# Identity products in thirteen waits of TensorE, group ends of the second attention from PSUM, and two gate tiles ahead of the last convolved ones

## The chip, the cores and the metric

The kernel runs on one core of one Trainium2 chip. A time is the device time of one execution in microseconds (us); the span of a profiled execution is the time between its first and last recorded instruction. The core's engines are TensorE (PE; its weight loads are listed as PEld), VectorE (DVE), ScalarE (ACT), GpSimd (POOL) and SyncE (SP, which here only starts transfers). Each runs a program of its own, and the programs meet at semaphores.

## The reference

Six residual layers over 512 tokens of 512 features (`x`), with a context of 8192 rows (`ctx`). Each layer takes the layer norm of `x` and adds to `x`:

```
x = x + cross_attention(norm(x), ctx, mask)   # s0: softmax over 8192 keys, masked after the softmax
x = x + retention(norm(x))                    # s1: state = lam*state + v; q*state; norm; silu gate
x = x + quantised_ffn(norm(x))                # s2: 4-bit weight blocks, 16-bit activations scaled by a global maximum
x = x + memory_attention(norm(x), ctx)        # s3
x = x + mamba2(norm(x))                       # s4: conv of 4 taps, silu, scan, gate silu(z), rms norm
x = x + ternary_ffn(norm(x))                  # s5: 8-bit rows, ternary weights, conv of 3 taps between two products
```

In s3 the memory of a token is the context row of its highest score, and then 16 heads of 32 attend over the 512 memories:

```
qp     = q @ Wq.T;  idx = argmax(qp @ ctx.T);  mem = ctx[idx]
mk, mv = split(mem @ Wkv.T)
out    = softmax(heads(qp) @ mk.T / sqrt(32)) @ mv;  out @ Wc.T
```

In s4, `silu(z)` is the gate and `xBC = silu(conv(xBC))` holds the convolved tiles.

## The kernel before

The work is written out by hand, stage by stage (s0 to s5), one function for each engine and stage. What an engine does stands in the order of its code; it waits with `wait_ge` on a semaphore that another engine raises. All 512 tokens are in four tiles of 128 rows (`NT`), the features in four tiles of 128 (`DT`).

Wide products are made as three float16 products of 128x512 (high by high, high by low, low by high): `matmul_split`, L248 to L250, for the projections, L796 to L798 for the product of probabilities and context in s0, L1628 to L1630 for the scores of s3. PSUM has eight banks `PS[:, b, :]` of 128x512 float32.

At the end of each stage VectorE adds the product to a tile of `x` (L223, L225) and norms it (L205 to L211); `turn_tile` (L234) then has TensorE transpose the normed tile, ScalarE and VectorE copy and split it into `XT` (L288), and the first product of the next stage follows. These places, and those where a scale, a maximum or a sum crosses partitions, are where TensorE waits.

s0: `COLMAX` is spread over the partitions (L782), then the Fori over `PAIRS` makes the products, each context chunk with its low part `CLO` split by VectorE (L688). s1: the mean of the output (L950), 32 sums of one column (L956), spreads of the token scale (L961), then the float32 output product (L968). s2: turns, gate and up projections, then the down projection, which waits for the hidden tiles that VectorE quantises (L1244, L1246, the maximum; L1254, the first slice out).

s3 starts with a float32 projection (L1613). After the scores come the entries: `entry(e)` (L1681) makes logits whose maximum VectorE takes (L1555); the last entry of a head group (L1686) spreads that maximum. Then 64 units: `shifted(n)` (L1697) makes the logits of a head and a tile of 128 memories, ScalarE takes the exponential (L1504) into one of 16 buffers, and GpSimd adds them up (L1463). `weigh(b)` (L1709) multiplies four units with the values into bank 6. Four heads make a group, 16 units; at its end `sums(g)` (L1720, L1724) brings the sum of the exponentials into bank 7, and VectorE's `weighted(g)` divides bank 6 by it. In three groups of four it copies both banks first, so that TensorE may write them again; the last divides from PSUM. `weigh` lags the units by 9.

s4: after the split the small `dt` products come (40 of 16 columns, L248 to L250), then ten convolved tiles (VectorE, L1974; ScalarE's silu, L1899) and the eight gate products, which ScalarE takes out of two banks in turn with a silu (L1902). The order of ScalarE's code: all convolved silus, then all gate silus. `L2110` is a product on `IDENTB`, a bfloat16 identity, with a broadcast operand.

s5: the turns, a first projection (L2281), a scale spread over the partitions (L2296) and the second projection (L2302).

Of the kernel before, what the change touches and what calls it, by code (L numbers as in the profile page):

```python
# [29 lines left out]
P = 128  # L30
# [84 lines left out]
def perceiver_kernel(nc, a, out):  # L115
    ctx = ExitStack()
    with ctx:
# [120 lines left out]
        def keep_warm(pe, bank, rounds):  # L238


            with pe.Fori(0, rounds):
                for _ in range(8):
                    pe.matmul(PS[:, bank, 0:P], IDENT[:, :], ONES[:, :], start=True, stop=True)

# [488 lines left out]
        def s0_pe(pe):  # L733
# [50 lines left out]
            ins.then_inc(pe_marks, 1)  # L784
            with pe.Fori(0, PAIRS) as i:
                for b in range(2):
                    for j in range(CH):
                        k = (i * 2 + b) * CH + j
                        if j == 0:
                            pe.wait_ge(s0_c_hi, i * 2 + b + 1 + AHEAD_SPLIT)  # L790
                            pe.wait_ge(s0_c_lo, i * 2 + b + 1 + AHEAD_SPLIT)
                        pe.wait_ge(s0_p_hi, k + 1)
                        pe.wait_ge(s0_p_lo, k + 1)
                        for t in range(NT):
                            cols = slice(t * P, (t + 1) * P)
                            pe.matmul(PS[:, t, :], PHI[:, j, cols], CHI[:, b, j, :], start=False, stop=False)  # L796
                            pe.matmul(PS[:, t, :], PHI[:, j, cols], CLO[:, b, j, :], start=False, stop=False)  # L797
                            ins = pe.matmul(PS[:, t, :], PLO[:, j, cols], CHI[:, b, j, :], start=False, stop=False)  # L798
                        ins.then_inc(s0_pv, 1)
# [6 lines left out]
            ins.then_inc(pe_marks, 1)  # L806

# [11 lines left out]
            for t in range(NT):  # L819
# [5 lines left out]
                if t:  # L825
                    turn_tile(pe, 1, t - 1)
            turn_tile(pe, 1, NT - 1)

# [101 lines left out]
        def s1_pe(pe):  # L930
# [19 lines left out]
            pe.matmul(PS[:, 4, :], MEANW[:, :], Y[:, DT - 1, :], start=False, stop=True).then_inc(pe_marks, 1)  # L950
            pe.wait_ge(s1_gate, 2)
# [11 lines left out]
            ins.then_inc(pe_marks, 1)  # L963
            for e, rows in ((0, (0, 1)), (1, (0, 1)), (2, (0,)), (3, (0,)), (2, (1,)), (3, (1, 2, 3))):
# [295 lines left out]
        def s2_pe(pe):  # L1260
            for t in range(NT):
                turn_tile(pe, 2, t)
            for n, psum in enumerate((s2_gt_psum, s2_up_psum)):
# [16 lines left out]
            pe.wait_ge(s2_w_lo, WEIGHTS + AHEAD_LOW)  # L1280
            for g in range(F0T):
# [7 lines left out]
            for t in range(NT):  # L1289
                turn_tile(pe, 3, t)  # L1290
# [43 lines left out]
        LAG = 4  # L1334
# [174 lines left out]
        def s3_dve(dve, link):  # L1509
# [56 lines left out]
            def weighted(g):  # L1566

                dve.wait_ge(s3_pv, 4 * g + 4)
                dve.wait_ge(pe_marks, PE_MARK[f"s3_sums{g}"])
                if g < GROUPS - 1:  # L1570
                    dve.tensor_copy(DEN, PS[:, 7, :]).then_inc(s3_den, 1)
                    dve.tensor_copy(ATTT[:, g, :], PS[:, 6, :]).then_inc(s3_den, 1)
                    dve.wait_ge(s3_den, 3 * g + 2)
                    dve.reciprocal(DEN, DEN).then_inc(s3_den, 1)
                    dve.wait_ge(s3_den, 3 * g + 3)
                    dve.tensor_tensor(ATTT[:, g, :], ATTT[:, g, :], DEN, ALU.mult).then_inc(s3_attt, 1)
                    dve.wait_ge(s3_attt, g + 1)
                else:
                    dve.reciprocal(DEN, PS[:, 7, :]).then_inc(s3_den, 1)
                    dve.wait_ge(s3_den, 3 * g + 1)  # L1580
                    dve.tensor_tensor(ATTT[:, g, :], PS[:, 6, :], DEN, ALU.mult).then_inc(s3_attt, 1)
# [25 lines left out]
        def s3_pe(pe):  # L1607
# [92 lines left out]
            def weigh(b):  # L1700
# [5 lines left out]
                if m == 0 and g:  # L1706
                    pe.wait_ge(s3_den, 3 * (g - 1) + 2)
# [5 lines left out]
            def sums(g):  # L1713
# [3 lines left out]
                if g:  # L1717
                    pe.wait_ge(s3_den, 3 * (g - 1) + 1)
# [13 lines left out]
            for n in range(UNITS + 6):  # L1732
# [7 lines left out]
                if n >= 9 and n % 4 == 1:  # L1740
                    weigh((n - 9) // 4)
            sums(GROUPS - 1)
            pe.wait_ge(s3_attt, DT)
            for t in range(NT):
# [4 lines left out]
                if t:  # L1749
                    turn_tile(pe, 4, t - 1)  # L1750
            turn_tile(pe, 4, NT - 1)

# [131 lines left out]
        def s4_act(act, link):  # L1884
# [8 lines left out]
            for g in range(CVT + 2):  # L1893
                if g < CVT:
                    act.wait_ge(s4_conv_psum, g + 1)
                    act.activation(XBC[:, g, 3:], PS[:, g % 4, :], ACT.Copy, scale=1.0 / W_UP).then_inc(s4_conv_in, 1)
                if g >= 2:
                    act.wait_ge(s4_conv, g - 1)
                    act.activation(CV[:, g - 2, :], CV[:, g - 2, :], ACT.Silu).then_inc(s4_cv, 1)  # L1899
            for g in range(2 * NT):  # L1900
                act.wait_ge(s4_z_psum, g + 1)
                act.activation(ZG[:, g // 2, (g % 2) * 512:(g % 2 + 1) * 512], PS[:, 4 + g % 2, :],  # L1902
                               ACT.Silu, scale=1.0 / W_UP).then_inc(s4_z, 1)
            act.wait_ge(dve_marks, DVE_MARK["s4_la"])
# [153 lines left out]
        def s4_pe(pe):  # L2058
# [106 lines left out]
            for t in range(1, NT):  # L2165
                turn_tile(pe, 5, t)
# [103 lines left out]
        def s5_pe(pe):  # L2270
# [27 lines left out]
            ins.then_inc(pe_marks, 1)  # L2298
            for g in range(F1T - LAST):
# [69 lines left out]
```

## Time and profile before

| | before |
|---|---|
| times of three runs | 1157.22 (median), 1149.74, 1835.84 us |
| the profiled execution | 1148.62 us, span 1146.9 us |
| TensorE busy | 1020.6 us (89%), 4756 products |
| VectorE busy | 818.7 us (71%) |
| ScalarE busy | 489.6 us (43%) |
| GpSimd busy | 417.8 us (36%) |
| TensorE's mean granted clock | 0.949 of full speed |

The granted clock of the page's 40 slices reads 9999999999999999789778999999979999989898, in tenths. A busy share is an average over six stages that are limited by different engines. In the rows below, a product's length is the time that it spends in the array; the next one starts before it ends, so the rate is read from the starts.

### The profile page before, as it was taken

The page shows a single profiled execution, that of the slowest core. Times are in us where ns is not written, and L with a number is a line of the kernel's source. Part 1 is how long each engine was busy: PE and PEld are TensorE (multiplying, and loading weights), DVE is VectorE, ACT ScalarE, POOL GpSimd, SP SyncE. Part 2 cuts the span into 40 slices and gives each one's busy share as a digit, 9 for nine tenths or more (in the row PEclk, how much of TensorE's full clock was granted, in tenths as well). Part 3 has the DMA queues.
Part 4 walks back from the last instruction along what each step waited for, and adds up shares of the span by engine and source line. Part 5 has one row for each costly group of instructions (what it writes and reads, how often), then busy time and mean ns, then how long its engine had stood idle before and what let it go on. Part 6 is the DMA issues. An engine that isn't in the chain of part 4 may idle for free.

```text
span 1146.9 us, 14403 instructions
## 1 busy us (share of the span) xinstructions
PE 1020.6 (89%) x4756; PEld 483.0 (42%) x4756; DVE 818.7 (71%) x1178; ACT 489.6 (43%) x731; POOL 417.8 (36%) x229
## 2 busy tenths in 40 slices
PE   7999999899999889699457999999988779888796
PEld 3444444344444334344123444444732135466353
DVE  5476666799999266685873299999478557476796
ACT  2345555666666537047761110100035514355163
POOL 4278777200000833000020377766128820084003
PEclk9999999999999999789778999999979989999898
DMA  6145555533442535120010335446100100000001
GB/s 231 76 136 185 189 172 163 177 110 146 146 139 80 208 144 211 61 92 1 0 74 15 130 143 201 185 179 173 37 1 1 44 32 1 0 1 1 2 1 37
DMA packets 41828, 112.61 MB, mean 98 GB/s; under 512 B 4512, under 2 KB 15296, under 8 KB 35648
## 3 DMA queue, kind: packets, MB, share of 16 engines
q1 hardware_dynamic: 38592, 101.13, 25.1%
q10 hardware_dynamic: 2880, 9.96, 2.6%
q0 software_dynamic: 320, 1.05, 0.3%
q8 instruction: 21, 0.34, 0.1%
q14 instruction: 15, 0.12, 0.0%
HBM read 103.18 MB, written 7.34 MB: 96 GB/s over the span
## 4 chain that ended last, share of the span: by engine, by line
PE 74%; DVE 15%; issue 5%; ACT 3%; POOL 2%; DMA 0%; DVEq 0%; SPq 0%; POOLq 0%; ACTq 0%
PE PS L796 5%; PE PS L797 5%; PE PS L798 5%; PE PS L766 5%; PE PS L1628 5%; PE PS L768 5%; PE PS L1630 5%; PE PS L1629 5%; PE PS L767 5%; PE PS L248 4%; PE PS L249 4%; PE PS L250 4%; DVE arena L1974 2%; PE PS L738 1%; PE PS L1746 1%
## 5 line engine op out<-in xcount | busy, mean ns | idle before, releaser
L796 PE MATMUL PS<-arena 128*128 128x512 f16 x256 | 97.7, 382 | 3.6 <-DVE arena L676 3.6
L766 PE MATMUL PS<-arena 128*128 128x512 f16 x256 | 97.1, 379 | 2.0 <-DVE arena L615 2.0
L1628 PE MATMUL PS<-arena 128*128 128x512 f16 x256 | 97.1, 379 | 1.8 <-DVE arena L1512 1.8
L797 PE MATMUL PS<-arena 128*128 128x512 f16 x256 | 97.9, 382 | 0.0
L798 PE MATMUL PS<-arena 128*128 128x512 f16 x256 | 97.8, 382 | 0.0
L1630 PE MATMUL PS<-arena 128*128 128x512 f16 x256 | 97.1, 379 | 0.0
L767 PE MATMUL PS<-arena 128*128 128x512 f16 x256 | 97.1, 379 | 0.0
L1629 PE MATMUL PS<-arena 128*128 128x512 f16 x256 | 97.1, 379 | 0.0
L768 PE MATMUL PS<-arena 128*128 128x512 f16 x256 | 97.1, 379 | 0.0
L622 DVE TENSOR_TENSOR arena<-PS,arena 128x512 f32<-128x512 f32 x64 | 43.6, 681 | 58.0 <-ACT arena L546 58.0
L480 POOL TENSOR_TENSOR arena<-arena 128x2048 f16<-128x2048 f32 x16 | 66.0, 4127 | 38.5 <-ACT arena L539 38.1
L248 PE MATMUL PS<-arena 128*128 128x512 f16 x112 | 43.8, 391 | 33.4 <-DVE arena L1254 28.5
L248 PE MATMUL PS<-XT,arena 128*128 128x512 f16 x184 | 71.4, 388 | 2.0 <-DVE XT L288 2.0
L249 PE MATMUL PS<-XT,arena 128*128 128x512 f16 x184 | 71.6, 389 | 0.0
L250 PE MATMUL PS<-XT,arena 128*128 128x512 f16 x184 | 71.3, 387 | 0.0
L546 ACT ACTIVATE arena<-PS 128x512 f32 (+1 forms) x64 | 38.0, 594 | 77.5 <-PE PS L768 77.5
L563 ACT ACTIVATE arena<-arena,MASK 128x512 f16 (+1 forms) x64 | 46.2, 722 | 54.3 <-PE PS L798 49.1
L1436 POOL TENSOR_TENSOR arena<-arena 128x2048 f16<-128x2048 f32 x16 | 65.4, 4089 | 1.3
L865 POOL TENSOR_SCALAR XN<-XN 128x2048 f32<-128x2048 f32 x1 | 1.9, 1901 | 164.8 <-ACT arena L589 164.8
L1474 ACT ACTIVATE XN<-XN 128x580 f32<-128x580 f32 x16 | 10.9, 678 | 118.2 <-DMA XN<-in_WinT 118.2
L676 DVE SCALAR_TENSOR_TENSOR arena<-arena,MASK 128x512 f16<-128x512 f16 (+1 forms) x64 | 48.0, 751 | 9.6 <-ACT arena L563 8.6
L217 ACT ACTIVATE STD<-MV,EPSC 128x1 f32<-128x1 f32 x24 | 7.1, 295 | 108.2 <-DVE MV L207 108.1
(368 smaller groups left out, 2437.4 us busy)
## 6 DMA issues: line engine op xcount, KB each, us to landing
arena<-in_ctxT SPq DMA_DIRECT2D x32, 1024.0 KB, 6.4
arena<-in_ctx SPq DMA_DIRECT2D x16, 1024.0 KB, 5.2
arena<-in_w ACTq DMA_DIRECT2D x8, 1024.0 KB, 5.3
arena<-in_w SPq DMA_DIRECT2D x8, 1024.0 KB, 4.8
XN<-in_ffnGU SPq DMA_DIRECT2D x16, 384.0 KB, 3.3
XN<-in_WinT SPq DMA_DIRECT2D x16, 290.0 KB, 5.0
gu_hi<-arena SPq DMA_DIRECT2D x16, 192.0 KB, 3.4
gu_lo<-arena SPq DMA_DIRECT2D x16, 192.0 KB, 3.5
```

The lines of the kernel that those rows point to most:

```text
L248: pe.matmul(out, w_hi, m_hi, start=(c == 0), stop=False)
L249: pe.matmul(out, w_hi, m_lo, start=False, stop=False)
L250: return pe.matmul(out, w_lo, m_hi, start=False, stop=(c == n - 1))
L766: pe.matmul(bank, CHI[:, b, e, cols], QHI[:, e, :], start=(e == 0), stop=False)
L767: pe.matmul(bank, CHI[:, b, e, cols], QLO[:, e, :], start=False, stop=False)
L768: ins = pe.matmul(bank, CLO[:, b, e, cols], QHI[:, e, :], start=False, stop=(e == DT - 1))
L796: pe.matmul(PS[:, t, :], PHI[:, j, cols], CHI[:, b, j, :], start=False, stop=False)
L797: pe.matmul(PS[:, t, :], PHI[:, j, cols], CLO[:, b, j, :], start=False, stop=False)
L798: ins = pe.matmul(PS[:, t, :], PLO[:, j, cols], CHI[:, b, j, :], start=False, stop=False)
L1628: pe.matmul(bank, QHI3[:, e, cols], CHI3[:, b, e, :], start=(e == 0), stop=False)
L1629: pe.matmul(bank, QHI3[:, e, cols], CLO3[:, b, e, :], start=False, stop=False)
L1630: ins = pe.matmul(bank, QLO3[:, e, cols], CHI3[:, b, e, :], start=False, stop=(e == DT - 1))
```

## The change

A helper `fill(pe, bank, times)` makes 128x512 products of the bfloat16 identity with itself into a PSUM bank that nobody reads, and it is called in thirteen waits: 225 products in all. The down projection of s2 gets two more waits ahead of its 20. In s3, `weighted(g)` divides straight from PSUM in all four groups; `weigh` of a new group waits for the product of the division (`s3_attt`), `sums` for the reciprocal, and `weigh` lags the units by 13. In s4, ScalarE takes gate tiles 0 and 1 ahead of the convolved tiles 8 and 9.

```diff
+        def fill(pe, bank, times):
+            for _ in range(times):
+                pe.matmul(PS[:, bank, :].rearrange("p (a b) -> p a b", b=P), IDENTB[:, :],
+                          IDENTB[:, :].unsqueeze(1).to_broadcast([P, 4, P]), start=True, stop=True)
...
@@ s0, after the spread of COLMAX (L782), and after the sums (L805)
+            fill(pe, 7, 12)
...
+            fill(pe, 7, 8)
@@ s0's end
+            fill(pe, 4, 9)
             turn_tile(pe, 1, NT - 1)
+            fill(pe, 4, 4)
@@ s1, after the last mean (L950), and after the spread (L961)
+            fill(pe, 7, 6)
...
+            fill(pe, 2, 6)
@@ s2_pe
+            fill(pe, 0, 28)
             for t in range(NT):
                 turn_tile(pe, 2, t)
+            fill(pe, 4, 4)
...
             pe.wait_ge(s2_w_lo, WEIGHTS + AHEAD_LOW)
+            pe.wait_ge(s2_up, F0T)
+            pe.wait_ge(s2_tmag, NT + 2 * F0T + 2 * SLICES - 1)
+            fill(pe, 0, 20)
             for g in range(F0T):
...
             for t in range(NT):
+                fill(pe, 4 if t else 0, 8)
                 turn_tile(pe, 3, t)
@@ s3_dve, weighted(g)
-                if g < GROUPS - 1:
-                    dve.tensor_copy(DEN, PS[:, 7, :]).then_inc(s3_den, 1)
-                    dve.tensor_copy(ATTT[:, g, :], PS[:, 6, :]).then_inc(s3_den, 1)
...
+                dve.reciprocal(DEN, PS[:, 7, :]).then_inc(s3_den, 1)
+                dve.wait_ge(s3_den, g + 1)
+                dve.tensor_tensor(ATTT[:, g, :], PS[:, 6, :], DEN, ALU.mult).then_inc(s3_attt, 1)
+                dve.wait_ge(s3_attt, g + 1)
@@ s3_pe
                 if m == 0 and g:
-                    pe.wait_ge(s3_den, 3 * (g - 1) + 2)
+                    pe.wait_ge(s3_attt, g)
...
                 if g:
-                    pe.wait_ge(s3_den, 3 * (g - 1) + 1)
+                    pe.wait_ge(s3_den, g)
...
                 if e in (1, 2):
                     values(e + 1)
+                elif e:
+                    fill(pe, 6, 3)
-            for n in range(UNITS + 6):
+            for n in range(UNITS + BEHIND):
...
-                if n >= 9 and n % 4 == 1:
-                    weigh((n - 9) // 4)
+                if n >= BEHIND and n % 4 == 1:
+                    weigh((n - BEHIND) // 4)
             sums(GROUPS - 1)
+            fill(pe, 5, 18)
...
+            fill(pe, 4, 10)
             turn_tile(pe, 4, NT - 1)
+            fill(pe, 4, 4)
@@ s4_act
+            for g in range(CVT):
+                act.wait_ge(s4_conv_psum, g + 1)
+                act.activation(XBC[:, g, 3:], PS[:, g % 4, :], ACT.Copy, scale=1.0 / W_UP).then_inc(s4_conv_in, 1)
+                if g >= 2:
+                    s4_conv_silu(g - 2)
+            for g in range(2 * NT):
+                s4_gate_silu(g)
+                if g < 2:
+                    s4_conv_silu(CVT - 2 + g)
@@ s4's end
+            turn_tile(pe, 5, 1)
+            fill(pe, 4, 6)
+            turn_tile(pe, 5, 2)
+            fill(pe, 4, 18)
+            turn_tile(pe, 5, 3)
+            fill(pe, 4, 3)
@@ s5, after the spread of the scale (L2296)
+            fill(pe, 5, 7)
```

In the changed kernel the lines behind the helper stand seven or more lines later: L248 to L250 are its L255 to L257, and its L249 is the identity product.

TensorE at the end of s2, where the last two of the normed tiles are turned and s3's float32 projection (L1613, after: L1624) follows. Before:

```order
L234 MATMUL PS<-IDENT,XN 128x128 [waits ln_xn]
L234 MATMUL PS<-IDENT,XN 128x128 x3
L234 MATMUL PS<-IDENT,XN 128x128 [waits ln_xn]
L234 MATMUL PS<-IDENT,XN 128x128 x3
L1613 MATMUL PS<-XT,arena 128x512 [waits xt_ready,w_in3]
```

After:

```order
L249 MATMUL PS<-IDENTB 128x512 x8
L234 MATMUL PS<-IDENT,XN 128x128 [waits ln_xn]
L234 MATMUL PS<-IDENT,XN 128x128 x3
L249 MATMUL PS<-IDENTB 128x512 x8
L234 MATMUL PS<-IDENT,XN 128x128 [waits ln_xn]
L234 MATMUL PS<-IDENT,XN 128x128 x3
L1624 MATMUL PS<-XT,arena 128x512 [waits xt_ready,w_in3]
```

The last two turns are shown; eight identity products now stand ahead of each of the four.

TensorE in s3's units, at the start of a new head group: L1686 (after: L1697) spreads a group's maximum, L1697 (L1708) is a unit, L1709 (L1720) a weigh. Before:

```order
L1686 MATMUL PS<-IDENT,arena 4x128 [waits s3_taken_even,s3_taken_odd]
L1686 MATMUL PS<-IDENT,arena 4x128 x3
L1709 MATMUL PS<-arena 32x512 [waits s3_den,s3_p]
L1709 MATMUL PS<-arena 32x512 x3
L1697 MATMUL PS<-arena 128x512 [waits s3_p] x4
L1709 MATMUL PS<-arena 32x512 [waits s3_p]
L1709 MATMUL PS<-arena 32x512 x3
L1697 MATMUL PS<-arena 128x512 [waits s3_p] x2
```

After:

```order
L1697 MATMUL PS<-IDENT,arena 4x128 [waits s3_taken_even,s3_taken_odd]
L1697 MATMUL PS<-IDENT,arena 4x128 x3
L1720 MATMUL PS<-arena 32x512 [waits s3_p]
L1720 MATMUL PS<-arena 32x512 x3
L1708 MATMUL PS<-arena 128x512 [waits s3_p] x4
L1720 MATMUL PS<-arena 32x512 [waits s3_attt,s3_p]
L1720 MATMUL PS<-arena 32x512 x3
L1708 MATMUL PS<-arena 128x512 [waits s3_p] x2
L1708 MATMUL PS<-arena 128x512 [waits s3_p,s3_qst]
```

The first weigh of the new group stood right behind the spread and waited for the copies (`s3_den`); now the last weigh of the old group stands there, and the new group's first one, four units later, waits for the division (`s3_attt`).

TensorE at the end of s3: L1720 and L1724 (after: L1731, L1735) are the last sums, L1746 (L1760) the output product. Before:

```order
L1709 MATMUL PS<-arena 32x512 [waits s3_p]
L1709 MATMUL PS<-arena 32x512 x3
L1709 MATMUL PS<-arena 32x512 [waits s3_p]
L1709 MATMUL PS<-arena 32x512 x3
L1720 MATMUL PS<-XT,ONES 32x512 [waits s3_den,s3_acc]
L1720 MATMUL PS<-XT,ONES 32x512 x3
L1724 MATMUL PS<-arena,ONES 32x512 x4
L1746 MATMUL PS<-arena 128x512 [waits s3_attt]
```

After:

```order
L1720 MATMUL PS<-arena 32x512 [waits s3_p]
L1720 MATMUL PS<-arena 32x512 x3
L1720 MATMUL PS<-arena 32x512 [waits s3_p]
L1720 MATMUL PS<-arena 32x512 x3
L1720 MATMUL PS<-arena 32x512 [waits s3_p]
L1720 MATMUL PS<-arena 32x512 x3
L1731 MATMUL PS<-XT,ONES 32x512 [waits s3_den,s3_acc]
L1731 MATMUL PS<-XT,ONES 32x512 x3
L1735 MATMUL PS<-arena,ONES 32x512 x4
L249 MATMUL PS<-IDENTB 128x512 x18
L1760 MATMUL PS<-arena 128x512 [waits s3_attt]
```

Three weighs stand without a unit between them where two did, and 18 identity products stand between the sums and the output product.

ScalarE in s4, at the end of the convolution: L1896 (after: L1923) takes a convolved tile's input out of PSUM, L1899 (L1913) is its silu, L1902 (L1918) a gate silu. Before:

```order
L1896 ACTIVATE arena<-PS 128x512
L1899 ACTIVATE arena<-arena 128x512
L1896 ACTIVATE arena<-PS 128x512
L1899 ACTIVATE arena<-arena 128x512 x3
L1902 ACTIVATE arena<-PS 128x512 x8
L1905 ACT_TABLE_LOAD
```

After:

```order
L1923 ACTIVATE arena<-PS 128x512
L1913 ACTIVATE arena<-arena 128x512
L1923 ACTIVATE arena<-PS 128x512
L1913 ACTIVATE arena<-arena 128x512
L1918 ACTIVATE arena<-PS 128x512
L1913 ACTIVATE arena<-arena 128x512
L1918 ACTIVATE arena<-PS 128x512
L1913 ACTIVATE arena<-arena 128x512
L1918 ACTIVATE arena<-PS 128x512 x6
L1931 ACT_TABLE_LOAD
```

The first gate silu moved ahead of the last two convolved silus, the second ahead of the last.

## Rows read from the trace of the kernel before

**Rows 1.** Stretches of 1.2 GHz by windows: us, engines' busy (count), PEclk, DMA; last, full clock

```profile
216.20:219.60 3.40, 3.40 (x9) 1.31 (x10) 3.29 (x6) 2.85 (x6) 0.00 (x0) 0.53 1.01 371
387.70:390.30 2.60, 2.60 (x7) 0.95 (x8) 1.83 (x3) 0.73 (x2) 2.52 (x3) 0.50 0.99 385
417.60:421.00 3.40, 3.40 (x9) 1.29 (x10) 3.37 (x5) 2.04 (x3) 0.00 (x0) 0.52 1.01 422
463.90:468.80 4.90, 4.90 (x6) 2.18 (x7) 4.17 (x6) 0.00 (x0) 0.00 (x0) 0.50 0.02 6
492.30:496.10 3.80, 3.79 (x9) 1.33 (x10) 3.77 (x5) 0.61 (x2) 0.00 (x0) 0.50 0.00 0
585.10:588.20 3.10, 3.10 (x8) 1.13 (x9) 1.57 (x3) 3.04 (x6) 0.00 (x0) 0.50 1.01 418
628.30:632.60 4.30, 4.30 (x5) 1.82 (x6) 0.00 (x0) 1.32 (x3) 0.00 (x0) 0.50 0.74 239
848.70:853.10 4.40, 4.40 (x11) 1.43 (x12) 3.87 (x4) 1.68 (x3) 0.00 (x0) 0.50 0.00 0
921.30:926.20 4.90, 4.90 (x6) 2.18 (x7) 0.00 (x0) 0.00 (x0) 0.00 (x0) 0.50 0.00 0
945.40:950.10 4.70, 4.70 (x41) 4.22 (x40) 0.22 (x1) 0.21 (x1) 2.24 (x2) 0.50 0.01 3
984.60:987.60 3.00, 2.97 (x8) 1.05 (x9) 2.60 (x10) 0.46 (x1) 0.00 (x0) 0.50 0.00 0
1083.40:1086.60 3.20, 3.19 (x8) 1.09 (x9) 1.65 (x3) 0.60 (x2) 0.00 (x0) 0.50 0.00 0
1128.20:1131.00 2.80, 2.77 (x7) 1.03 (x8) 2.80 (x6) 2.80 (x5) 2.80 (x5) 0.50 0.00 0
240.00:340.00 100.00, 100.00 (x465) 45.18 (x463) 94.51 (x126) 65.39 (x88) 0.00 (x0) 1.00 0.38 134
```

**Rows 2.** Timeline, TensorE: start, length, instruction, [idle before <- releaser]

```profile
621.63 0.66 PE L234 MATMUL PS<-IDENT,XN 128*128 128x128 f32 x4 [2.05 <-DVE XN L211]
...
624.35 1.11 PE L234 MATMUL PS<-IDENT,XN 128*128 128x128 f32 x4 [2.06 <-DVE XN L211]
...
646.33 0.39 PE L1628 MATMUL PS<-arena 128*128 128x512 f16 x1 [1.82 <-DVE arena L1512]
...
1004.34 0.38 PE L2110 MATMUL PS<-FUTUREB,IDENTB 128*128 128x512 bf16 x1
```

**Rows 3.** Timeline at the start of stage s0's products

```profile
225.41 2.29 DVE L688 TENSOR_TENSOR arena<-arena 128x2048 f16<-128x2048 f32 x1
...
228.24 0.38 PE L796 MATMUL PS<-arena 128*128 128x512 f16 x1
```

**Rows 4.** Chain that ended last, stage s1: the spread of the scale

```profile
460.19 2.09 PE PS L961 x8
```

**Rows 5.** Timeline, TensorE, start of stage s2

```profile
487.59 3.87 PE L234 MATMUL PS<-IDENT,XN 128*128 128x128 f32 x16 [7.20 <-DVE XN L1167]
```

**Rows 6.** Timeline, VectorE, the last maximum but one of stage s2's product

```profile
577.08 1.22 DVE L1246 TENSOR_REDUCE SM<-arena 128x1 f32<-128x1024 f32 x1
```

**Rows 7.** Timeline, TensorE, gate products of stage s4

```profile
984.63 0.61 PE L248 MATMUL PS<-arena,XT 128*128 128x512 f16 x1 [2.29 <-ACT arena L1902]
```

**Rows 8.** Timeline of stage s3's group ends, TensorE and VectorE

```profile
873.43 0.68 DVE L1571 COPY arena<-PS 128x512 f32<-128x512 f32 x1
...
874.86 1.07 PE L1709 MATMUL PS<-arena 128*32 128x512 f32 x8 [0.16 <-DVE arena L1572]
...
878.13 1.12 DVE L1576 TENSOR_TENSOR arena<-arena 128x512 f32<-128x512 f32 x1
...
907.93 1.07 PE L1709 MATMUL PS<-arena 128*32 128x512 f32 x8
...
917.16 3.36 DVE L1579 RECIPROCAL arena<-PS 128x512 f32<-128x512 f32 x1 [4.51 <-PE PS L1724]
...
920.55 0.69 DVE L1581 TENSOR_TENSOR arena<-PS,arena 128x512 f32<-128x512 f32 x1
```

More of the change, by code:

```diff
@@ L1333, in perceiver_kernel @@
         MSHIFT = 64.0
-        LAG = 4
+        BEHIND = 13
         s3_clip = sem("s3_clip")
@@ L1569, in weighted @@
                 dve.wait_ge(pe_marks, PE_MARK[f"s3_sums{g}"])
-                if g < GROUPS - 1:
-                    dve.tensor_copy(DEN, PS[:, 7, :]).then_inc(s3_den, 1)
-                    dve.tensor_copy(ATTT[:, g, :], PS[:, 6, :]).then_inc(s3_den, 1)
[L1573 to L1581, printed above, removed]
+                dve.reciprocal(DEN, PS[:, 7, :]).then_inc(s3_den, 1)
+                dve.wait_ge(s3_den, g + 1)
+                dve.tensor_tensor(ATTT[:, g, :], PS[:, 6, :], DEN, ALU.mult).then_inc(s3_attt, 1)
+                dve.wait_ge(s3_attt, g + 1)
             def take_entry(e):
@@ L1892, in s4_act, with s4_conv_silu, s4_gate_silu @@
             act.activation(DTE, DTE, ACT.Ln, bias=1.0).then_inc(act_marks, 1)
[L1893 to L1900, printed above, removed]
+            def s4_conv_silu(g):
+                act.wait_ge(s4_conv, g + 1)
+                act.activation(CV[:, g, :], CV[:, g, :], ACT.Silu).then_inc(s4_cv, 1)
+            def s4_gate_silu(g):
                 act.wait_ge(s4_z_psum, g + 1)
@@ L2164, in s4_pe @@
             project_rows(3)
-            for t in range(1, NT):
-                turn_tile(pe, 5, t)
+            turn_tile(pe, 5, 1)
[4 more added lines that the diff above has]
+            fill(pe, 4, 3)
         W1B = view(53 * K, [DT, FF1], F16)
```

## Prediction

> **What bounds the kernel now.** I read the page first: TensorE is busy for most of the span, yet its granted clock is not 9 in every slice. Then the timeline of TensorE gave the starts of its 128x512 products, and the windows put a row on each stretch where they start at twice the usual distance. The reader is to see in [rows 1] that thirteen stretches have a granted clock of 0.50 to 0.53, TensorE's level of 1.2 GHz, while TensorE is busy for all of each; the last row is a stretch at 1.00 (2.4 GHz) with 465 products in 100 us, so one each 0.215 us. At the lower level it is 0.43 (8 starts in 3.4 us). All thirteen stretches follow a pause of TensorE: in [rows 2] a turn of four transposes takes 0.66 after an idle 2.05, and 1.11 after one more idle 2.06. A pause of 1.82 elsewhere left the first product at 0.39, full clock. The fourth row there is the kernel's own product on the bfloat16 identity: 0.38 at full clock, like any other, so an identity product costs 0.215 to issue.
>
> Where TensorE bounds a stretch of length L at half clock, full clock saves L/2. Everything below is summed against the profiled execution (1148.62, of which 1146.9 is span). That is 8.6 under the median of the three times, 1157.22, and 1.1 under the lowest.
>
> **The products, place by place**, in the order of [rows 1]; each first with L/2.
> - s0, 3.4: 1.7. The twelve products (2.6) lie in the wait. But the fourth key tile's second part needs the split that ends at 225.41 + 2.29 = 227.70 and TensorE reaches that tile at 228.24 [rows 3], so little over 0.4 can be kept. Bounds 0.4 and 1.7; I take 0.4, the row being right there.
> - s0 after the sums, 2.6: 1.3. Retention's start, 3.4: 1.7 (nine and four products, 2.8, in pauses ahead of and behind the last turn).
> - s1's scale, 4.9: 2.45, and half of the eight spreads of 2.09 [rows 4], 1.05, so 3.5 at most. The spreads end at 462.28 and the next product starts at 463.9: six products fit (1.3), but not at half clock (2.6), which would cost 1.0. The 32 one-column sums between the two fills keep TensorE at little work. Bounds -1.0 and 3.5; I take 1.5, between, nearer to the upper since the second fill alone shortens the pause.
> - s2's start, 3.8: 1.9. The 28 products take 6.0 of a wait of 7.20 [rows 5].
> - s2 down: 3.1 gives 1.55. The fill waits for the maximum that ends at 577.08 + 1.22 = 578.30 [rows 6]; 20 products take 4.3, or 8.6 at half clock, when they would end at 586.9 against 585.10. What is queued behind that new wait on TensorE is only the down projection, which needs a later step anyway. Bounds -1.8 and 1.55; I take 1.5.
> - s3's start, 4.3: 2.15. Eight products (1.7) ahead of each turn; the turns come each 2.72 (the starts in [rows 2]), so they fit at full clock. 2.2.
> - s3's entries, 4.4: 2.2. GpSimd is idle in that stretch and its sums, which come after, wait for the first weights, so all of it moves. VectorE is busy 3.87 of the 4.4, so at least 0.5. I take 2.2, the chain there being TensorE's.
> - s3's end, 4.9: 2.45. 18 products (3.9) beside the reciprocal and product, 3.36 + 0.69 [rows 8]: 2.4.
> - s4's first small products, 4.7: 2.35. All 40 are 16 columns, bound by weight loads (4.22 of 4.70); the transposes of [rows 2], loads with short products too, go from 1.11 to 0.66, so these halve nearly as well. 2.3, bounds 1.5 and 2.35. The convolution behind moves as a whole.
> - s5's start, 3.2: 1.6. s5 second projection, 2.8: 1.4, but its seven products (1.5, at half clock 3.0) may end 1.5 late. I take 1.2, bounds -1.5 and 1.4.
>
> **The gate tiles.** TensorE waits 2.29 for the first gate silu [rows 7], which stands behind the convolved silus 8 and 9 on ScalarE; with gate tiles 0 and 1 ahead of them the gate products run through. That removes the 2.29 and half of the 3.0 at half clock behind it: 3.8. The moved convolved silus are read by VectorE and TensorE after the gate products end, so their 0.6 each is covered.
>
> Sum of gains: 0.4 + 1.3 + 1.7 + 1.5 + 1.9 + 1.5 + 2.2 + 2.2 + 2.4 + 2.3 + 1.6 + 1.2 + 3.8 = 24.0.
>
> **The group ends of s3.** Two copies of 0.68 go, but the copies were what let TensorE on: its first weigh of the next group stood behind the second copy only (0.16 idle, at 874.86 [rows 8]). Now that weigh waits for the whole division. So each weigh is put four units later, and the last weigh of a group takes the place of the old first one, at 874.86: the sums are complete at 875.9, not before 873.43; the reciprocal (3.36) and product (0.69) end at 880.0, against 878.13 + 1.12 = 879.25. VectorE's next entries, queued behind, and through them the units that GpSimd paces, come 0.7 later, in two groups: 1.4. At the end it costs more: weigh 11 takes the slot at 907.93, ends at 909.0, the division ends at 913.1; then come weighs 12 to 15 (4 x 1.07) and the sums (2 x 1.07), 919.5 against 917.16: 2.3. Together 3.7; the two 0.7 partly hide behind GpSimd's own pace, so I take 3.1. Bounds: a loss of 3.7, and a gain of 3 x (2 x 0.68 + 0.43) = 5.4 if VectorE's shorter ends were all that counts and the later weighs nothing.
>
> The row of 0.69 is a product with one operand in PSUM, when GpSimd had no more sums; those of 1.12 had both in SBUF, beside GpSimd. The Trainium skill (SBUF — State Buffer, section "Who interferes with whom") says that a VectorE instruction with two SBUF inputs contends with a GpSimd instruction that reads SBUF, and one with at most one such input does not. By that rule the 0.69 holds beside GpSimd; without it the product would take 1.12 and two groups would end 0.4 later each, 0.8 in all. No row of this trace shows the new form beside GpSimd.
>
> Forecast: 1148.6 - 24.0 + 3.1 = 1127.7, so **1128**.
>
> **The rivals.**
> 1. VectorE is as late. In the stretches at 216, 417, 464, 492 and 849 it is busy 3.29 of 3.40, 3.37 of 3.40, 4.17 of 4.90, 3.77 of 3.80 and 3.87 of 4.40 [rows 1], so a faster TensorE would meet it. For it: these shares. Against: TensorE ran without a pause there, and much of VectorE's work is for what comes later. It takes away 0.4 + 1.7 + 1.5 + 1.9 + 2.2 = 7.7: 1135.
> 2. The group ends save: the later weighs hide behind GpSimd's pace and the shorter ends count. 1127.7 - 3.1 - 3 x 1.36 = 1120.5, so 1121. Against: the tail's 2.3 has nothing beside it.
> 3. Slower: the identity products don't bring the clock up. Then at 0.43 each the eight ahead of a turn take 3.4, with the turn's 1.11 4.5, over the 2.72 from which it decides: 1.8 x 4 = 7.3 late. The 28 take 12.0 of 7.2: 4.8 late; the 18 take 7.7 of 4.05: 3.7 late. No stretch gets faster, of the gains only 2.3 stays: 1148.6 + 7.3 + 4.8 + 3.7 + 3.1 - 2.3 = 1165; the ten fills at the entries (1.3 each) could bring 1178. Against: the row of 0.38 shows that such a product fills TensorE like a real one, and the clock was 1.00 wherever real ones ran on.
> 4. The gate tiles come no earlier, because the silu ahead of gate 0 is as late as silu 9: 3.8 stay, 1132.
>
> **How the numbers follow.** Forecast 0.45, rival 1 0.25, rival 2 0.20, rival 3 0.06, rival 4 0.04. The range goes down from rival 2 by the upper bounds at 216, s1's scale and s5 (1.3 + 2.0 + 0.2, and 1 for rounding), to 1116, and up from rival 1 by the lower bounds of s2 down, s5 and s1's spread (3.3 + 2.7 + 1.0), with 1 for the group ends, to 1143. Outside lie rival 3 and tails, about 0.15. Two per cent, about what a measurement of this kernel can tell from no change, is 1134 under the median shown, but 1126.7 under the lowest time, near which the profiled execution stands. My forecast lies between these bounds, so half of its weight and all of rival 2 and some of rival 4 are faster, rival 1 is within 2%, and slower has most of rival 3: faster 0.50, same 0.45, slower 0.05.
>
> **What would show it.** The thirteen stretches at clock 1.00, and their products 0.22 apart; the turns of s3 0.66 each; no wait of TensorE for the first gate silu; VectorE's division of the last group starting 2 to 3 after TensorE's last unit more than it did; the product from PSUM near 0.69 beside GpSimd. I am wrong if fills show 0.63 each or turns start later, or if TensorE's waits for VectorE grow by what its products lost.

## The result, and the profile after

The changed kernel took 1139.23 us (median of four, 1138.12 to 1140.73), the kernel before, in the same comparison, 1153.48 (median of four, with 1148.51 the lowest). The ratio is 0.9897, with a 95% interval of 0.9852 to 0.9941, and leaves out one slow run of before, of 1835.84: 1.0% faster. The time lies in the predicted range, but the gain is less than half of the one forecast: between the profiled executions 7.9, where 24.0 - 3.1 = 20.9 were forecast. The profiled execution took 1140.73, with a span of 1139.0 and a mean clock of 0.971 (0.949 before). In the page's row of granted clock of before, the slice at 918 to 946 us has 8 and that at 1004 to 1032 us has 9; the row under the times before has these two the other way round.

The same places as in [rows 1], in the windows of the changed kernel. The columns and the order are those of [rows 1]; the times have moved, and the eighth window holds added products as well:

```profile
218.90:220.90 2.00, 1.96 (x10) 0.93 (x11) 1.88 (x4) 1.73 (x4) 0.00 (x0) 1.00 0.93 345
390.30:391.70 1.40, 1.40 (x7) 0.63 (x8) 1.40 (x3) 0.68 (x2) 1.40 (x2) 1.00 1.01 369
420.10:422.10 2.00, 1.96 (x10) 0.92 (x11) 2.00 (x4) 0.72 (x3) 0.00 (x0) 1.00 1.01 422
465.90:468.30 2.40, 2.40 (x7) 1.14 (x7) 2.34 (x4) 0.00 (x0) 0.00 (x0) 1.00 0.00 0
491.60:493.50 1.90, 1.90 (x9) 0.87 (x10) 1.90 (x4) 0.59 (x2) 0.00 (x0) 1.00 0.00 0
582.40:584.10 1.70, 1.70 (x8) 0.77 (x9) 0.69 (x1) 1.67 (x4) 0.00 (x0) 1.00 1.00 419
623.80:625.80 2.00, 1.99 (x5) 1.04 (x6) 0.00 (x0) 1.34 (x3) 0.00 (x0) 1.00 0.60 164
841.20:844.70 3.50, 3.37 (x16) 1.18 (x15) 3.50 (x4) 1.97 (x4) 0.00 (x0) 1.00 0.00 0
925.00:927.40 2.40, 2.40 (x6) 1.20 (x7) 0.00 (x0) 0.00 (x0) 0.00 (x0) 1.00 0.02 7
946.50:949.00 2.50, 2.50 (x41) 2.27 (x40) 0.15 (x1) 0.00 (x0) 2.35 (x2) 1.00 0.00 0
981.00:982.70 1.70, 1.70 (x9) 0.75 (x8) 1.55 (x4) 0.65 (x2) 0.00 (x0) 1.00 0.00 0
1078.10:1080.20 2.10, 2.10 (x8) 0.51 (x9) 1.61 (x3) 0.57 (x2) 0.00 (x0) 1.00 0.00 0
1121.70:1123.20 1.50, 1.50 (x8) 0.73 (x8) 1.50 (x4) 1.50 (x3) 1.50 (x3) 1.00 0.00 0
```

Each of the thirteen stretches is now at 1.00, the level of 2.4 GHz. The small products of s4 (the tenth row) went from 4.70 to 2.50.

So the loss is elsewhere, and the starts of equal instructions in the two traces say where. Their difference is the lead that the changed kernel has at that point; the change of the lead across a place is what the place brought:

| place | forecast | measured |
|---|---|---|
| s0, products | 0.4 | 0.2 |
| s0, after the sums | 1.3 | 0.0 |
| s1's start | 1.7 | 1.7 |
| s1's scale | 1.5 | 1.4 |
| s2's start | 1.9 | 2.1 |
| s2 down | 1.5 | 1.1 |
| s3's start | 2.2 | 3.0 |
| s3's entries | 2.2 | 2.0 |
| s3's group ends | -3.1 | -12.4 |
| s3's output | 2.4 | 2.5 |
| s4's small products | 2.3 | 2.4 |
| gate tiles | 3.8 | 4.0 |
| s5's start | 1.6 | 1.4 |
| s5, second projection | 1.2 | 1.4 |

The gains add up to 23.1 before rounding, where 24.0 were forecast. Take off 12.4, and 2.7 that this execution was later already by the end of s0's first wait, at work that stands ahead of the first added product: 8.0, and the two profiled executions differ by 7.9.

The 12.4 is the stretch from GpSimd's first sum to VectorE's last reciprocal in s3: 62.8 before (854.3 to 917.16), 75.3 after (845.57 to 920.85). Its windows, cut at GpSimd's first sum of each group and at the end of its last sum; before:

```profile
854.30:869.00 14.70, 12.60 (x65) 3.74 (x63) 10.27 (x10) 9.44 (x17) 14.69 (x12) 0.99 0.00 1
869.00:887.90 18.90, 14.99 (x84) 4.15 (x88) 15.56 (x14) 9.55 (x17) 15.35 (x13) 1.00 0.01 1
887.90:903.80 15.90, 11.29 (x70) 2.72 (x66) 8.56 (x7) 9.33 (x17) 15.29 (x12) 1.00 0.00 1
903.80:915.00 11.20, 9.50 (x59) 1.69 (x59) 6.40 (x4) 7.29 (x12) 10.39 (x8) 1.00 0.12 25
```

and in the changed kernel:

```profile
845.60:860.30 14.70, 11.22 (x55) 3.34 (x55) 10.91 (x10) 9.39 (x17) 14.70 (x13) 1.00 0.00 1
860.30:883.20 22.90, 18.75 (x84) 4.75 (x88) 13.15 (x11) 9.56 (x17) 14.94 (x13) 0.78 0.00 1
883.20:902.30 19.10, 15.07 (x70) 3.14 (x66) 6.98 (x5) 9.34 (x17) 14.90 (x13) 0.74 0.01 2
902.30:914.40 12.10, 8.55 (x41) 1.32 (x33) 4.05 (x2) 4.93 (x9) 9.87 (x8) 0.78 0.00 1
```

Where no group ends, nothing changed: 14.7 and 14.7, GpSimd without a pause. Each group that contains an end is longer, by 4.0, 3.2 and 0.9, and the tail behind the last sum by another 4.3 (6.4 against 2.2). GpSimd's busy time is the same (some 55), so it waits (14.4 in these four windows, 5.0 before), and TensorE's clock, 0.99 to 1.00 in this whole stretch before, falls to 0.74 to 0.78 from the second window on. Over the whole stretch TensorE is busy 60.1 with the 286 products that took it 50.3 before. The timeline of TensorE has the pauses; one at each of the three group ends:

```profile
873.22 1.04 PE L1692 MATMUL PS<-arena 96*128 96x512 f16 x2 [3.54 <-DVE arena L1581]
...
893.60 1.94 PE L1720 MATMUL PS<-arena 128*32 128x512 f32 x8 [1.97 <-DVE arena L1591]
...
913.19 1.94 PE L1720 MATMUL PS<-arena 128*32 128x512 f32 x8 [2.41 <-DVE arena L1591]
```

L1591 is the product of the division, L1581 the shift row that is queued behind it on VectorE, L1720 the first weigh of the next group, 1.94 long at half clock where the weigh at 874.86 in [rows 8] took 1.07 after waiting 0.16. The entry of the first group end waited for the shift row before as well:

```profile
880.02 0.61 PE L1681 MATMUL PS<-arena 96*128 96x512 f16 x2 [2.70 <-DVE arena L1562]
```

That pause grew by 0.8 only. What grew more is how late the row comes: 12.2 after GpSimd's first sum of the group (860.27 to 872.49), 10.3 before (869.03 to 879.29).

Two places brought little or nothing for another reason. In s0 the products run through at full clock, and then TensorE waits for VectorE's split:

```profile
230.80 0.38 PE L804 MATMUL PS<-arena 128*128 128x512 f16 x1 [1.34 <-DVE arena L695]
```

The other is s0 after the sums. The timeline of the changed kernel there, GpSimd and VectorE:

```profile
404.81 4.07 POOL L879 TENSOR_TENSOR arena<-arena 128x2048 f16<-128x2048 f32 x1
...
407.26 1.89 DVE L211 TENSOR_SCALAR XN<-X,MV,RSTD 128x512 f32<-128x512 f32 x1
```

The projections got their 1.3, but the first norm behind them now takes 1.89 and ends at 409.15, just after GpSimd's subtraction of weights (408.88), and the lead at the turn behind it is what it was ahead of the sums.

### The profile page after: what moved, and what is told of

Its sections match the earlier page's. It is cut to its first block, busy times and chain, and to the rows that moved or that the text cites. A ratio compares the mean times of both kernels' runs of the same rounds, so it can differ in the third digit from the quotient of the medians.

```text
span 1139.0 us, 14848 instructions
## 1 busy us (share of the span) xinstructions
PE 1055.0 (93%) x4981; PEld 498.2 (44%) x4981; DVE 813.6 (71%) x1172; ACT 490.0 (43%) x731; POOL 415.6 (36%) x229
## 4 chain that ended last, share of the span: by engine, by line
PE 77%; DVE 13%; issue 4%; ACT 3%; POOL 1%; DMA 0%; DVEq 0%; SPq 0%; ACTq 0%; POOLq 0%
PE PS L773 5%; PE PS L774 5%; PE PS L775 5%; PE PS L1639 5%; PE PS L1641 5%; PE PS L1640 5%; PE PS L255 5%; PE PS L257 5%; PE PS L256 5%; PE PS L804 5%; PE PS L805 5%; PE PS L806 5%; PE PS L745 1%; PE PS L1720 1%; PE PS L2311 1%
## 5 line engine op out<-in xcount | busy, mean ns | idle before, releaser
L773 PE MATMUL PS<-arena 128*128 128x512 f16 x256 | 97.7, 382 | 2.0 <-DVE arena L622 2.0
L1639 PE MATMUL PS<-arena 128*128 128x512 f16 x256 | 97.0, 379 | 1.8 <-DVE arena L1531 1.8
L804 PE MATMUL PS<-arena 128*128 128x512 f16 x256 | 97.0, 379 | 1.6 <-DVE arena L695 1.3
L774 PE MATMUL PS<-arena 128*128 128x512 f16 x256 | 97.8, 382 | 0.0
L775 PE MATMUL PS<-arena 128*128 128x512 f16 x256 | 97.7, 381 | 0.0
L1640 PE MATMUL PS<-arena 128*128 128x512 f16 x256 | 97.0, 379 | 0.0
L1641 PE MATMUL PS<-arena 128*128 128x512 f16 x256 | 97.0, 379 | 0.0
L805 PE MATMUL PS<-arena 128*128 128x512 f16 x256 | 97.0, 379 | 0.0
L806 PE MATMUL PS<-arena 128*128 128x512 f16 x256 | 97.0, 379 | 0.0
L249 PE MATMUL PS<-IDENTB 128*128 128x512 bf16 x225 | 57.7, 401 | 21.9 <-DVE SM L1259 21.9
L255 PE MATMUL PS<-XT,arena 128*128 128x512 f16 x184 | 69.7, 379 | 0.6 <-DVE XT L295 0.6
L256 PE MATMUL PS<-XT,arena 128*128 128x512 f16 x184 | 69.7, 379 | 0.0
L257 PE MATMUL PS<-XT,arena 128*128 128x512 f16 x184 | 69.7, 379 | 0.0
L1493 ACT ACTIVATE XN<-XN 128x580 f32<-128x580 f32 x16 | 10.9, 679 | 118.1 <-DMA XN<-in_WinT 118.1
L1523 ACT ACTIVATE arena<-PS 128x512 f32<-128x512 f32 x64 | 36.0, 593 | 40.4 <-PE PS L1708 36.2
```

The costliest lines, as they stand in the source:

```text
L255: pe.matmul(out, w_hi, m_hi, start=(c == 0), stop=False)
L256: pe.matmul(out, w_hi, m_lo, start=False, stop=False)
L257: return pe.matmul(out, w_lo, m_hi, start=False, stop=(c == n - 1))
L773: pe.matmul(bank, CHI[:, b, e, cols], QHI[:, e, :], start=(e == 0), stop=False)
L774: pe.matmul(bank, CHI[:, b, e, cols], QLO[:, e, :], start=False, stop=False)
L775: ins = pe.matmul(bank, CLO[:, b, e, cols], QHI[:, e, :], start=False, stop=(e == DT - 1))
```

## The experiments

Theory D at the start: the new group ends cost the missing time, because TensorE is held for the division. Rivals: L, the longer lag does it; F, the identity products delay something; C, it is TensorE's clock. All ratios are to the kernel before on the same chip; its medians there were 1149.9 to 1151.3, so a difference between the medians of two runs on different chips is good to some 1.5 us; "stretch" is again from GpSimd's first sum to the last reciprocal of s3, in the profiled execution.

**old_ends**: all products and gate tiles, group ends as before.

```diff
-                dve.reciprocal(DEN, PS[:, 7, :]).then_inc(s3_den, 1)
+                if g < GROUPS - 1:
+                    dve.tensor_copy(DEN, PS[:, 7, :]).then_inc(s3_den, 1)
+                    dve.tensor_copy(ATTT[:, g, :], PS[:, 6, :]).then_inc(s3_den, 1)
...
-                    pe.wait_ge(s3_attt, g)
+                    pe.wait_ge(s3_den, 3 * (g - 1) + 2)
...
-        BEHIND = 13
+        BEHIND = 9
```

> All identity products and the gate tiles, but the group ends of s3 as before (two copies, the first weigh of a group waits for the copies, lag of 9 units). Theory D (the group ends cost some 14 us, since TensorE is held for the whole division and falls to 1.2 GHz in the pauses) and rival L (the same 14 us, but from the longer lag): 1125 to 1128 us, 2.0 to 2.2% under before, clock 1.00 all through the units. Rival F (the group ends cost the 3 us of the prediction, and the identity products delay something in s3): 1136.

Measured: 1128.58, ratio 0.9818 (0.9788 to 0.9848); stretch 64.3. F falls: the products are not what costs. D and L both stand.

**ends_alone**: the kernel before with the new group ends, no identity product, the old gate order.

```diff
-            for _ in range(times):
+            for _ in range(0):
...
-            pe.wait_ge(s2_up, F0T)
-            pe.wait_ge(s2_tmag, NT + 2 * F0T + 2 * SLICES - 1)
```

> The kernel before with the new group ends of s3 alone (division from PSUM, lag 13), without identity products and with the old order of the gate tiles. Theory D and rival L: 10 to 14 us slower than before, 1159 to 1163, with windows of the units at a clock of about 0.8. Rival F: 3 us slower, 1152.

Measured: 1160.81, ratio 1.0091 (1.0066 to 1.0115); stretch 75.1. The cost, 10.9, is the same with and without the products (1139.23 - 1128.58 = 10.7).

**lag_alone**: the changed kernel with both copies and the wait for them, but a lag of 13.

> The changed kernel with the two copies back, the first weigh of a group waiting for the copies, but the lag of 13 units kept. Theory D: the copies let TensorE on, so within 3 us of the kernel with the old ends, 1126 to 1129. Rival L: the lag is the cost, so like the changed kernel, 1137 to 1140.

Measured: 1135.10, ratio 0.9871 (0.9846 to 0.9897), between the two expectations; stretch 71.2. The longer lag costs 6.5 by itself. The waits of TensorE (releaser, total, times, longest):

```profile
PE PS L1700 <- DVE arena L1581: 5.9, 2, 5.1
PE PS L1716 <- DMA arena<-arena: 4.7, 1, 4.7
```

In old_ends the same two are 3.5 and 1.9, so they grew by 5.2, and the stretch by 6.9. The old group's last weigh comes four units later, so do the end of its sum and the division, and behind that the shift row and its transfer.

**psum_lag9**: the changed kernel with the lag of 9.

```diff
-        BEHIND = 13
+        BEHIND = 9
```

> The changed kernel with the division from PSUM, but the lag back to 9 units. Theory D: the first weigh stands four units earlier and is held for the whole division in each group, so as slow as the changed kernel or slower, 1139 to 1146. Rival L: the lag was the cost, so 1126 to 1130.

Measured: 1141.57, ratio 0.9923 (0.9896 to 0.9949); stretch 76.9. Dividing straight from PSUM costs 13.0 against old_ends, with no longer lag at all. So the lag of 13 does not hide the division; it exchanges some of one loss for the other.

**after_warm**: the changed kernel, identity products also in the pauses of the units.

```diff
+                if e > PAIRS_G + 2 and i == 1:
+                    fill(pe, bank + 1, 16)
...
+                if m == 0 and g >= 2:
+                    fill(pe, 3, 10)
...
+                fill(pe, 7, 6)
                 pe.wait_ge(s3_acc, added(16 * g + (11 if last else 15)))
...
+                    if n > 45:
+                        fill(pe, 3, 1)
```

> The changed kernel with further identity products in the pauses of s3's units: 16 ahead of the entry that follows a group's shift, 6 ahead of the sums, 10 ahead of the first weigh of groups 2 and 3, one behind each unit after the 45th. Theory C (what the group ends cost beyond the 3 us of the prediction is TensorE's clock, which fell to 0.67 to 0.82 in the units): the clock comes back to about 1.00 and the time to 1131 or 1132. Theory W (the waits for the division and the later shift row themselves cost it, the clock only follows): 1136 to 1140 although the clock is back.

Measured: 1138.32, ratio 0.9893 (0.9877 to 0.9910); stretch 73.0. The windows of this kernel from GpSimd's first sum:

```profile
841.50:914.50 73.00, 69.25 (x380) 21.35 (x381) 35.10 (x28) 35.62 (x63) 54.45 (x44) 1.00 0.07 26
```

The clock is 1.00 and the stretch only 2.3 shorter (the median 0.9). C falls as the whole cause: at full clock, too, the first weighs of groups 2 and 3 start at 889.31 and 906.30, where the divisions that they wait for end at 889.04 and 906.24. But the run doesn't say how much the clock is worth, since some of the added products stand in no pause: the six ahead of the last sums hold these from 910.99 to 912.39, when all that they need is there, and GpSimd pauses 1.15 ahead of its first sum of the second group, where it had no pause in the changed kernel. With the 1.4 alone I estimate the clock's share of the 12.4 at 3.7 or more; the rest of the split stays open.

**half_ends**: one copy only (bank 6), the reciprocal from bank 7, lag 9.

```diff
+                    dve.tensor_copy(ATTT[:, g, :], PS[:, 6, :]).then_inc(s3_den, 1)
+                    dve.reciprocal(DEN, PS[:, 7, :]).then_inc(s3_den, 1)
+                    dve.wait_ge(s3_den, 2 * g + 2)
+                    dve.tensor_tensor(ATTT[:, g, :], ATTT[:, g, :], DEN, ALU.mult).then_inc(s3_attt, 1)
...
+                    pe.wait_ge(s3_den, 2 * (g - 1) + 1)
```

> All identity products and the gate tiles, lag 9; at a group's end VectorE copies bank 6 alone, then takes the reciprocal straight from bank 7, so the first weigh waits for one copy and the division ends one copy (0.68) earlier. If the length of VectorE's work at a group's end is what delays the shift row behind it: 1 to 2 us under the kernel with the old ends, 1127. If GpSimd's pace hides it: the same 1128.6.

Measured: 1126.55, ratio 0.9799 (0.9776 to 0.9823), the fastest median of all; stretch 61.8. Its interval overlaps that of old_ends, and half_noB below, with the same s3, has a stretch of 64.3, so it isn't told apart from old_ends. The two executions of the same s3 differ in the product of the division, which has both inputs in SBUF here: at the first group end it took 0.69 in half_ends, and a sum of GpSimd that began 0.02 later took 1.79; in half_noB it took 1.82 beside a sum of 1.26.

**split_ends**: both copies, the division in three parts behind the next entries.

```diff
+                if n % 16 in (10, 12, 14) and n > 16:
+                    divide(n // 16 - 1, (n % 16 - 10) // 2)
```

> As the kernel with the old ends (both copies, lag 9, all products, gate tiles), but the division of the first three groups is made in three parts behind the next entries, so that the shift row of the next group isn't queued behind it. If that queue is what TensorE and GpSimd wait for at a group's end: their waits of 2 to 3 us in two groups go, 1123 to 1126. If GpSimd's pace is the bound anyway: 1128 to 1129.

Measured: 1129.85, ratio 0.9815 (0.9798 to 0.9831); stretch 67.8. The shift row is no longer behind the division, but the maxima of the entries are (TensorE waits 3.8 for them, 0.9 in old_ends), and the sum of it is no gain.

**gate_alone**: the kernel before with the new order of the gate tiles.

> The kernel before with the gate tiles 0 and 1 ahead of the convolved tiles 8 and 9, and nothing else. By the prediction: 3.8 us under before (the wait of 2.29 and half of 3.0 at half clock). If the gate silu is held by the silu ahead of it: no change.

Measured: 1148.68, ratio 0.9983 (0.9962 to 1.0003). In its trace the lead changes by 4.0 across the gate products (from 3.8 behind to 0.2 ahead) and TensorE no longer waits for a gate silu; the medians hold 2.7 of it, and their interval includes none.

**after_shift** and **lag_shift**: the changed kernel and lag_alone with VectorE's work at a group's end placed behind the shift row.

```diff
-                if n % 16 == 6 and n > 16:
+                if n % 16 == 9 and n > 16:
                     weighted(n // 16 - 1)
```

> The changed kernel, but VectorE takes the next group's shift row ahead of the division at a group's end (the last weigh of the group and that shift stand together on TensorE). Theory Q (with the lag of 13, the division starts later and the shift row queued behind it holds TensorE and the transfer of the row): the pause of 3.5 ahead of the entry goes, the stretch from GpSimd's first sum to the last reciprocal falls from 75 to some 68, 1132. Theory H (TensorE is held at the new group's first weigh for the division, whatever stands ahead on VectorE): 73 to 76, 1137 to 1140.

> As above with the two copies back (lag 13, first weigh waits for the copies alone). Theory Q: the pause of 5.1 and the wait of 4.7 for the row's transfer go, the stretch falls from 71 to 64 or 65, 1128 to 1129. If the lag costs by itself (the exponentials wait for a weigh that is only three units ahead): 69 to 71, 1133 to 1135.

Measured: after_shift 1141.39, ratio 0.9916 (0.9890 to 0.9942), stretch 77.6; lag_shift 1133.51, ratio 0.9847 (0.9819 to 0.9874), stretch 68.5. The waits of TensorE in after_shift:

```profile
PE PS L1720 <- DVE arena L1591: 9.6, 3, 3.9
...
PE PS L1692 <- DVE arena L1581: 1.6, 2, 0.8
```

The pause ahead of the entry is gone (3.5, now 0.8), and the first weigh of all three groups now waits for the division instead (3.3, 3.9 and 2.5). Theory Q falls for the changed kernel: with the row out of the way, TensorE comes to the next thing that the division holds. For the lag alone the place of the row is a part only, 1.6 of 6.5. In the trace of lag_shift the wait has moved to the next thing in VectorE's queue: TensorE waits 5.5 (5.0 of it once) for the maxima of the entries, now behind the division, where it waited 0.9 in lag_alone. How the rest of the lag's cost is made up stays open.

**half_noB**: half_ends without the eight products after s0's sums.

> The kernel that copies bank 6 alone, without the eight products ahead of s0's output projections. In the changed kernel these gave TensorE 1.4 there, and it was gone at the next norm, which took 1.89 where it took 0.55. If GpSimd's subtraction of weights, which ends at the same time either way, is what that norm waits for: stretch 1.4 slower at the projection, norm 0.55 again, and no difference behind it. If not: 1.4 slower to the end.

Measured: one run, 1128.32. VectorE's first norm there and GpSimd's subtraction:

```profile
401.47 4.08 POOL L878 TENSOR_TENSOR arena<-arena 128x2048 f16<-128x2048 f32 x1
405.65 0.55 DVE L211 TENSOR_SCALAR XN<-X,MV,RSTD 128x512 f32<-128x512 f32 x1
```

The norm starts when the subtraction has ended and takes 0.55. Across the projections the lead changes by +1.3 with the products (half_ends) and by -0.3 without; at the turn behind the norm the change is 0.0 with them and still -0.3 without, one execution each. So of the 1.7 that the products gave at the projections 0.3 was left behind the norm.

**after_double** and **old_double**: a second reciprocal of 3.36, its result unused, in the first three groups of the changed kernel and of old_ends.

```diff
+                    link(dve.reciprocal(ATTT[:, g + 1, :], PS[:, 7, :]))
```

> The changed kernel with a second reciprocal of 3.36 us ahead of the real one in the first three groups (its result is not used). Theory H (the division stands in full on the path of TensorE's units in each of these groups): 3 x 3.36 = 10 us more than the changed kernel, 1148 to 1151. If GpSimd's pace or the lag of four more units hides the division: 0 to 3 us more, 1139 to 1142.

> The same second reciprocal in the kernel with the old ends (copies first, lag 9). If the copies take the division off TensorE's path: 0 to 3 us more than that kernel, 1129 to 1132. If the division counts there as well, through the entries that queue behind it on VectorE: 7 to 10 us more, 1136 to 1139.

Measured: after_double 1149.38, ratio 0.9985 (0.9960 to 1.0011), 10.2 over the changed kernel by the medians; stretch 81.9, 6.7 longer. old_double 1138.30, ratio 0.9883 (0.9842 to 0.9924), 9.7 over old_ends; stretch 73.7, 9.4 longer. Theory H holds for the changed kernel in the main: of the 10.1 added, 6.7 are paid in the stretch, and TensorE's waits for the product and the shift row rise from 4.4 and 4.3 to 11.2 and 7.7. That the copies take the division off the path is wrong, though: with them it is paid as well. There the waits of TensorE are for the row and its transfer (3.5 and 1.9 in old_ends):

```profile
PE PS L1701 <- DVE arena L1581: 6.5, 2, 5.7
PE PS L1717 <- DMA arena<-arena: 5.6, 1, 5.6
```

## Why the prediction was wrong

**The products were right** in their mechanism and, but for one, nearly term by term: thirteen stretches at 1.00, and 23.1 of 24.0, the gate tiles among them. Rival 1 (VectorE is as late) occurred in the first stretch alone, where TensorE then waits 1.34 for the split and 0.2 is left; the forecast had 0.4 for that reason (its rows give 228.24 - 227.70 = 0.54). In the third, fourth, fifth and eighth VectorE is still busy nearly throughout, and the gain came all the same. Rival 3 (the products don't bring the clock up) is refuted by the same rows. s1's scale went as its bounds had it: the spreads stayed at half clock (2.08), the six products behind them ran at half clock too (2.64) and delayed the next ones, whose full clock then gave more. That the term came out at 1.4, near the 1.5 taken, is the sum of these.

**The gate tiles were right**: 4.0 against 3.8, and no wait for the first gate silu; rival 4 falls.

**One small term failed**: s0 after the sums, 1.3, was taken as L/2 without asking what comes next. There the norm meets GpSimd's subtraction, whose end the products don't move, and 0.0 was left. The Trainium skill (SBUF — State Buffer, section "Who interferes with whom") says that a VectorE `tensor_scalar` in a two-port mode contends with GpSimd for a shared pair of ports and the second waits for the whole instruction; the trace agrees, 1.89 beside the subtraction and 0.55 behind it, though no row shows the mode.

**The step that failed** is the paragraph on the group ends of s3: "Together 3.7 ... so I take 3.1", with 3.7 as the worst bound. It measured 12.4 in the profiled stretch, 10.7 by the medians of the kernel with and without it. The direction was right, and so was the first thing it said: the copies were what let TensorE on. But it priced only what VectorE does later, 0.7 in two groups, put TensorE's wait for the division and the fall of its clock at nothing, and took for granted that the four units of extra lag give TensorE enough else to do while the division runs. They don't. Work behind the waiting instruction on TensorE's queue is every next unit; a unit that isn't made leaves ScalarE and then GpSimd without work, and GpSimd's pace, on which the 0.7 was to hide, is what stops. In the first group end the shift row comes 2.0 later, where 0.7 was forecast (among the work ahead of it is a weigh of 1.90 at half clock), and the entry behind it waits 3.5, 2.7 before. In the second the division ends 0.5 later, counted from GpSimd's first sum, about as forecast, and yet the weigh waits 2.0 for it; in the third it waits 2.4. Before, the first weighs of a group waited 0.16 at most, for a copy. The tail is the same error: the 2.3 for it assumed that weigh 12 follows the division with all units ahead already made, while the windows show 0.9 + 4.3 = 5.2 there. The sign named for it, the last division starting 2 to 3 later after the last unit, is absent: it starts 5.4 after it, 5.1 before, since the units themselves came late.

psum_lag9 and lag_alone show that the two halves of the edit each cost (13.0 and 6.5) and don't add; after_warm that the clock, which I hadn't considered in this stretch at all, is a part of the loss, by my estimate 3.7 or more, and not all of it; after_double that most of the division's length is paid in the changed kernel. How the 12.4 splits between the waits and the clock that falls with them isn't shown. Without the group ends the kernel takes 1128.58, so the group ends took back nearly half of what the rest gave.

**Rival 2** (the group ends save 3 x 1.36) was on the wrong side. Its one true point: the division is shorter by those copies, and half_ends, which keeps the copy that frees TensorE and drops the other, is no slower for it. The rule weighed there held: L1591 took 0.69 at 871.76 while GpSimd was at a sum, as the Trainium skill's section has it for one input in SBUF. It was priced at 0.8, on a path that lost 12.

**Chances.** No rival had the mechanism that came: a wait of TensorE for another engine's long instruction, with its units queued behind. The range reached 1139 only through rival 1, which came in one stretch of five, so that the time lies in the range is luck.

## What to carry to other kernels

In this kernel, filling a wait of TensorE with products on an identity was worth half of the half-clock stretch behind it, where TensorE bounded that stretch and nothing else ended at the same time; ask for each one what comes next. A copy out of PSUM that looks superfluous can be what releases the engine that fills PSUM: before removing it, list everything queued behind the instruction that will wait instead, and price the wait by the length of the work it now waits for, times the number of groups. Where two edits trade one wait for another, as lag and division here, lengthen the suspected work by a known amount: it tells whether it is on the path, though not by which wait.

## What I had not expected of the hardware

A normalising `TENSOR_SCALAR` of 128x512 took 1.89 us beside GpSimd's `TENSOR_TENSOR` and 0.55 behind it, and ended 0.27 after that instruction. Executions differ by up to 3 us ahead of the first edit: at s0's first wait, at 212 us, equal code was 2.6 later than before in five of the fourteen other profiled executions, 1.3 later in one and up to 0.7 earlier in the rest. In the five, 1.7 of it is TensorE's clock: behind a wait of some 2.0 its products at 42 us start 0.43 apart until 45.7, and 0.215 apart in before, behind the same wait. So a difference of 2 us between two kernels is read from the lead across its place and not from the whole time.
